# Attention with decay, first of four phases of a two-layer kernel: gates taken before the high part of the normed output, that part in four pieces, decay tables in two parts, the state updated with one kind of operation

## The reference, cut to what matters

```python
q = silu(x @ Wq); k = silu(x @ Wk); v = silu(x @ Wv)        # 2 x 1024 tokens, 16 heads of 32
D = exp(ld * (i - j)) * (i >= j)                             # inside a chunk of 128 tokens
q_decay = exp(ld * (i + 1)); k_decay = exp(ld * (127 - i)); chunk_decay = exp(ld * 128)
for each chunk:                                              # S starts at 0 in each sequence
    o = ((q @ k.T) * D) @ v + (q @ S) * q_decay
    S = chunk_decay * S + (k * k_decay).T @ v
gate = (x @ Wg1) @ Wg2
o = o * sigmoid(gate)
o = o * rsqrt(mean(o * o, per head) + 1e-5) * norm_w
x = layernorm(x + o @ Wo)
```

## Time and profile before

| | |
|---|---|
| median of 3 runs | 2120.58 us (2118.43 to 2133.62) |
| the profiled execution | 2121.79 us, its span 2120.0 us, granted clock 0.972 |
| attention phase | 0 to 378.3 us of the span |
| its round FIRST, chunks of t = 0 | 0 to 68.6, 68.6 to 95.2 us |
| a round NEXT and its chunks (t = 1) | 95.2 to 160.6, 160.6 to 180.4 us |
| the trunk | 378.3 to 2120.0 us |
| busy over the span | PE 88%, DVE 69%, POOL 61%, ACT 44% |

### The profile page before, as it was taken

One profiled execution on the slowest core, in us unless ns is written; L12 is line 12 of the kernel. 1 busy time (PEld: TensorE's weight loads), 2 busy tenths in 40 slices (PEclk: granted clock), 3 DMA queues, 4 the chain that ended last, 5 costly groups with the idle time before them and its releaser, 6 DMA issues. The chain is left out here.

```text
span 2120.0 us, 27907 instructions
## 1 busy us (share of the span) xinstructions
PE 1866.6 (88%) x9488; PEld 1184.6 (56%) x9488; DVE 1458.1 (69%) x1779; ACT 942.8 (44%) x1561; POOL 1296.3 (61%) x983
## 2 busy tenths in 40 slices
PE   8688897689998898888889889898998898999997
PEld 5556655357855555454545445454555455557785
DVE  2524414243337998798997999889989899994333
ACT  4333242344245555554546544564554544442212
POOL 4322520237327997788886998678878787782110
PEclk9899999899999999999999999999999999999999
DMA  6010100457667896778776886567657576764451
GB/s 207 22 40 2 41 20 11 150 179 267 227 214 265 322 328 235 252 268 295 267 266 224 314 297 223 193 231 253 224 205 274 192 251 225 260 222 159 166 210 61
DMA packets 132779, 427.28 MB, mean 202 GB/s; under 512 B 29184, under 2 KB 35840, under 8 KB 115872
## 3 DMA queue, kind: packets, MB, share of 16 engines
q1 hardware_dynamic: 132640, 425.53, 57.0%
HBM read 356.27 MB, written 69.21 MB: 201 GB/s over the span
## 5 line engine op out<-in xcount | busy, mean ns | idle before, releaser
L1489 POOL TENSOR_TENSOR h_times_c<-h_states,c_rep 128x512 f32<-128x512 f32 x512 | 669.7, 1321 | 177.7 <-PE scan_y L1137 118.4
L1271 ACT ACTIVATE decay<-delta_on_states,a_neg 128x512 f32<-128x512 f32 x512 | 353.7, 692 | 455.0 <-DVE h_states L1399 413.7
L1349 DVE TENSOR_TENSOR x<-x,y_or_aux 128x512 f32<-128x512 f32 x256 | 173.6, 678 | 221.8 <-PE y_or_aux L80 221.8
L1457 POOL TENSOR_TENSOR h_lo<-silu_in_h_lo,h_hi 128x512 fp32r<-128x512 f32 x128 | 171.3, 1338 | 248.0 <-ACT h_hi L1194 247.4
L1128 PE MATMUL du_spread<-stack,selectors 96*128 96x512 bf16 x512 | 203.0, 397 | 107.2 <-DVE d_b L1379 79.5
L1379 DVE TENSOR_TENSOR d_b<-du_spread,b_rep 128x512 f32<-128x512 f32 x384 | 254.7, 663 | 9.8 <-PE du_spread L1128 9.8
L78 PE MATMUL y_or_aux<-h_hi,w 128*128 128x512 f32 x512 | 241.6, 472 | 21.2 <-ACT b_rep L1236 8.9
L78 PE MATMUL gate<-x_hi,w 128*128 128x512 f32 x512 | 253.6, 495 | 7.4 <-POOL x_lo L1462 5.2
L1399 DVE TENSOR_TENSOR_SCAN h_states<-decay,h_last,d_b 128x512 f32<-128x512 f32 x192 | 245.1, 1277 | 12.8 <-ACT decay L1271 8.0
L78 PE MATMUL up<-x_hi,w 128*128 128x512 f32 x512 | 247.8, 484 | 0.0
L1399 DVE TENSOR_TENSOR_SCAN h_states<-decay,d_b 128x512 f32<-128x512 f32 x192 | 233.4, 1216 | 16.1 <-ACT decay L1271 11.7
(11 more groups left out here) (149 smaller groups left out, 3244.8 us busy)
## 6 DMA issues: line engine op xcount, KB each, us to landing
delta_on_states<-delta SPq DMA_DIRECT2D x256, 512.0 KB, 6.0
w<-w_split SPq DMA_DIRECT2D x112, 1024.0 KB, 6.7
w<-w_split SPq DMA_DIRECT2D x112, 512.0 KB, 6.4
w_split<-w_presplit SPq DMA_DIRECT2D x48, 512.0 KB, 5.6
w_split<-w SPq DMA_DIRECT2D x16, 1024.0 KB, 6.2
h_times_c<-in_w13a SPq DMA_DIRECT2D x16, 512.0 KB, 4.2
w_split<-w SPq DMA_DIRECT2D x16, 512.0 KB, 6.3
w_presplit<-in_w13b SPq DMA_DIRECT2D x32, 256.0 KB, 5.1
```

The lines of the kernel that those rows point to most:

```text
L1271: act.activation(da[:, s % ND], dring[:, s % NR], ACT.Exp, scale=a[:, column(s):column(s) + 1]).then_inc(s_da, 1)
L1349: dve.tensor_tensor(xt, xt, bank[:, :], ALU.add).then_inc(s_bank, 1)
L1457: pool.tensor_tensor(hl[:, idx % 4], sg[:, idx % 4], hh[:, idx % 4].bitcast(F32), ALU.subtract).then_inc(s_hl, 1)
L1489: pool.tensor_tensor(hc[:, s % NC_], hs[:, s % NH], crep[:, tile_of(s // SPO) % 2], ALU.mult).then_inc(s_hc, 1)
```

## The change

Five things are changed, all in the attention phase.
1. In FIRST, `decays` is cut in two: half of D, half of q_decay, k_decay and chunk_decay after the first take of k; the rest after the first take of v. Before it ran after the gate.
2. In NEXT, ACT takes the four gate products first and makes the high part of the normed output after them, in four casts of 128x512; DVE makes the low part in four pieces, each when its high piece is there; PE's first `wo` product waits for them piece by piece.
3. POOL makes the low part of the next x in four pieces.
4. The state's two operations per chunk become four `scalar_tensor_tensor` operations (128x32 each, one per feature tile), whose second tensor is in PSUM and whose scalar is one column of chunk_decay in SBUF.
5. Semaphores follow (counts in `on_hi`, `on_lo`, `attn_xl`; `state_scaled` is gone).

```diff
                     def outputs():
-                        if items is not TAIL:
-                            pe.wait_ge(s_ol, t)
                         for m in range(KD):
-                            project("wo", 3, m, onh, onl,
-                                    (lambda k: [by_piece(k, s_ol, NT, p_ol)]) if items is TAIL and m == 0 else None)
+                            project("wo", 3, m, onh, onl, (lambda k: [(s_ol, KD * rd.prev + k + 1)]) if m == 0 else None)
...
-                        pe.wait_ge(s_xl, t + 1)
+                        pe.wait_ge(s_xl, KD * t + 1)
...
-                def decays():
+                def decays(part):
...
-                    for j in range(HPT):
+                    for j in range(HPT)[2 * part:2 * part + 2]:
...
-                    for m in range(KD):
+                    for m in range(KD)[2 * part:2 * part + 2]:
...
                     def high_of_normed():
...
-                        act.wait_ge(s_on, KD * t + 1)
-                        act.wait_ge(s_pj, rd.done("v", CPT - 1))
-                        act.copy(onh[:, :, :], on[:, :, :]).then_inc(s_oh, 1)
+                        act.wait_ge(s_pj, rd.base if items is TAIL else rd.done("v", CPT - 1))
+                        for k in range(KD):
+                            act.wait_ge(s_on, KD * rd.prev + k + 2)
+                            act.copy(onh[:, k], on[:, k]).then_inc(s_oh, 1)
...
-                    take("k", kT, ACT.Silu)
+                    take("k", kT, ACT.Silu, ms=range(1))
+                    if items is FIRST:
+                        decays(0)
+                    take("k", kT, ACT.Silu, ms=range(1, KD))
...
-                    take("v", v, ACT.Silu)
+                    take("v", v, ACT.Silu, ms=range(1))
+                    if items is FIRST:
+                        decays(1)
+                    take("v", v, ACT.Silu, ms=range(1, KD))
+                    if items is NEXT:
+                        act.wait_ge(s_on, KD * t + 1)
+                    take("gate", sig, ACT.Tanh, 0.5)
                     if items is NEXT:
                         high_of_normed()
-                    take("gate", sig, ACT.Tanh, 0.5)
                     if items is FIRST:
-                        decays()
...
-                    pool.tensor_tensor(xl[:, :, :], x[:, :, bass.ts(t, TT)], xh[:, :, :].bitcast(F32),
-                                       ALU.subtract).then_inc(s_xl, 1)
+                    for k in range(KD):
+                        pool.tensor_tensor(xl[:, k], x[:, k, bass.ts(t, TT)], xh[:, k].bitcast(F32),
+                                           ALU.subtract).then_inc(s_xl, 1)
...
+                    def low_of_normed():
+
+                        for k in range(KD):
+                            dve.wait_ge(s_oh, KD * rd.prev + k + 1)
+                            dve.tensor_tensor(onl[:, k], on[:, k], onh[:, k].bitcast(F32), ALU.subtract).then_inc(s_ol, 1)
...
-                        dve.tensor_tensor(st[:, :, :], st[:, :, :], cdec[:, :].unsqueeze(2).to_broadcast([P, KD, HD]),
-                                          ALU.mult).then_inc(s_us, 1)
-                        dve.wait_ge(s_us, n + 1)
-                        dve.tensor_tensor(st[:, :, :], st[:, :, :], u_ps[:, :, :], ALU.add).then_inc(s_st, 1)
+                        for m in range(KD):
+                            mm = dve.scalar_tensor_tensor(out=st[:, m], in0=st[:, m], scalar=cdec[:, m:m + 1],
+                                                          in1=u_ps[:, m], op0=ALU.mult, op1=ALU.add)
+                        mm.then_inc(s_st, 1)
```

More of the change, by code:

```diff
@@ L139, in attention_phase @@
         s_o, s_og = p.sem("o_done"), p.sem("og_ready")
-        s_u, s_us, s_st = (p.sem(n) for n in ("update_done", "state_scaled", "state_ready"))
+        s_u, s_st = (p.sem(n) for n in ("update_done", "state_ready"))
         s_sq, s_sd, s_on = (p.sem(n) for n in ("squares", "head_rstd_ready", "on_ready"))
@@ L148, in attention_phase @@
         s_w0 = [p.sem(f"attn_w0_in_piece{k}") for k in range(KD)]
-        p_xh, p_xl, p_wh, p_wl, p_sq, p_oh, p_ol = (p.sem(f"attn_{n}_piece") for n in (
-            "xh", "xl", "w_hi", "w_lo", "squares", "on_hi", "on_lo"))
+        p_xh, p_xl, p_wh, p_wl, p_sq = (p.sem(f"attn_{n}_piece") for n in ("xh", "xl", "w_hi", "w_lo", "squares"))
         def by_piece(k, whole, count, piece):
@@ L422, in weight_high @@
                     act.copy(aw_hi[:, i], raws[i % 2][:, :, :]).then_inc(s_wh, 1)
-                def decays():
-                    act.wait_ge(s_sm, 96)
-                    act.wait_ge(s_const, 16)
-                    for j in range(HPT):
+                def decays(part):
+                    if part == 0:
+                        act.wait_ge(s_sm, 96)
+                        act.wait_ge(s_const, 16)
+                    for j in range(HPT)[2 * part:2 * part + 2]:
                         for m in range(KD):
@@ L432, in decays, with take @@
                                            scale=ldt[:, h:h + 1]).then_inc(s_dexp, 1)
-                    for m in range(KD):
+                    for m in range(KD)[2 * part:2 * part + 2]:
                         act.activation(qdec[:, m, :], const[:, C_POS:C_POS + P], ACT.Exp,
                                        scale=ldf[:, m:m + 1]).then_inc(s_dexp, 1)
-                    act.activation(kdec[:, :], kdec[:, :], ACT.Exp,
-                                   scale=const[:, C_REV:C_REV + 1]).then_inc(s_dexp, 1)
-                    act.activation(cdec[:, :], ldf, ACT.Exp, scale=float(CH)).then_inc(s_dexp, 1)
+                    if part == 0:
+                        act.activation(kdec[:, :], kdec[:, :], ACT.Exp,
+                                       scale=const[:, C_REV:C_REV + 1]).then_inc(s_dexp, 1)
+                        act.activation(cdec[:, :], ldf, ACT.Exp, scale=float(CH)).then_inc(s_dexp, 1)
                 def body(rd):
                     t, items = rd.t, rd.items
-                    def take(name, out, f, scale=1.0):
-                        for m in range(KD):
+                    def take(name, out, f, scale=1.0, ms=range(KD)):
+                        for m in ms:
                             act.wait_ge(s_pj, rd.done(name, m))
@@ L590, in body @@
                                                      in1=sq[:, m], op0=ALU.mult, op1=ALU.mult).then_inc(s_on, 1)
-                        if items is TAIL:
-                            for k in range(KD):
-                                dve.wait_ge(*by_piece(k, s_oh, NT, p_oh))
-                                dve.tensor_tensor(onl[:, k], on[:, k], onh[:, k].bitcast(F32), ALU.subtract)\
-                                   .then_inc(by_piece(k, s_ol, NT, p_ol)[0], 1)
+                    def low_of_normed():
+                        for k in range(KD):
+                            dve.wait_ge(s_oh, KD * rd.prev + k + 1)
+                            dve.tensor_tensor(onl[:, k], on[:, k], onh[:, k].bitcast(F32), ALU.subtract).then_inc(s_ol, 1)
                     def add_outputs():
@@ L604, in body @@
                     if items is TAIL:
+                        low_of_normed()
                         add_outputs()
```

9 lines of the change are left out of this document (removed).

## The result

The changed kernel took 2114.64 us (median of 14 runs) beside 2129.14 for the kernel before (median of 14): ratio 0.9942, 95% interval 0.9923 to 0.9961, that is 12 us less (8 to 16; the medians are 14.5 apart). Timed again on another chip it gave the same ratio, 0.9942 (0.9925 to 0.9960). The forecast was 11.3 us less than the profiled execution, which is 0.9947, and 2110 us in all. The kernel before ranges from 2118 to 2134 as in the three runs that I had seen, but the median of 14 is 2129.14, where that of the three was 2120.58: my forecast started too low.

What follows compares the result with a forecast made beforehand. It took waits in the attention phase as all the change could move, on POOL and ACT; the trunk keeps its length. Gains 5.5 + 1.3 + 4.5 = 11.3 us off 2121.79 gave 2110 us, range 2102 to 2119.

Steps and rivals of the forecast that it cites:

- The state, 5.5 us: First tile's first chunk: the new state operations do not wait for POOL, so the stall goes; 5.5 us gained.
- The decays, 1.3 us: First tile: with decays in two parts, scores start at 68.1 instead of 68.62 and take about 0.9 less; 1.3 us gained.
- PE slips 2.0 us: First tile, PE's fourth k product: its bank is freed at 33.0 instead of 31.0, after the first decays part.
- Rival (b): First tile: three more table loads cost 1.4 us more each, so POOL starts still later; 2113 us, 8%.
- rival (d): First tile: DVE's mask and q_decayed slip between POOL's stages cheaply, PE stays at 2.4 GHz; 6 us more, 2104, 13%.
- The table loads gone from the loop, zero: ACT in the loop: removed loads lay in covered waits, so nothing gained; without that cover 2.6 us a tile.
- The loop, 4.5 us: Other three tiles: low pieces let POOL's last butterfly end earlier; 1.5 us a tile taken, 4.5 in all.
- my two cases: POOL's last butterflies in the loop: first low piece comes between them, gain 1.24 us a tile, or misses, 1.9.
- rival (c): Loop: low pieces hold POOL as long as before, or PE falls to 1.2 GHz more often; gain 0, 2115, 18%.
- The trunk: From 378.3 us on, 1741.7 us long: keeps its length; a change over 3 us would show the forecast wrong.
- Rival (a): Chunks of the first three tiles: new state operations wait for POOL too; 47 us lost, 2163 us, 4%.

Runs made afterwards that it cites:

- state only: Kernel before, with only the state's two operations per chunk replaced by four that read the update from PSUM; ratio to before 0.9979.
- decays only: Kernel before, with only the decays cut in two parts, after the first takes of k and of v; ratio to before 1.0060.
- load kept: Kernel before with the decays' split, plus one table load put back ahead of the next tile's cast in the loop; ratio to before 1.0012.
- all but decays: Changed kernel with the decays in one piece again, after the gate; ratio to before 0.9932, taken again 0.9939.
- gates only: Kernel before, with only the loop's gates taken first and the normed output's high and low parts in four pieces; ratio to before 0.9976.
- x low pieces only: Kernel before, with only POOL's low part of x in four operations and PE's wait for them; ratio to before 0.9987.

## Why the prediction was right, by its own steps

**The state, 5.5 us.** Measured 5.5 (state only: 94.55 to 89.08). My own numbers gave 5.6 (84.86 less 79.26). The mechanism was right: these operations, with one tensor in SBUF, one in PSUM and a column in SBUF, took 0.71 or 0.72 us beside POOL and without it. Four operations cost 0.71 us, where I took 1.0. What I missed is that cutting POOL's operation gives the same in the first tile; two parts of the change remove the same stall, so their gains alone (5.5 each by the second gated output) don't add.

**The decays, 1.3 us.** The gain was not found, and one step was off in size: "PE slips 2.0 us". PE waited 2.04 us, but in the first profile fell to 1.2 GHz behind it and slipped 3.8; POOL's second load and its butterflies came 4.7 later instead of 2.0. In the second profile the clock stayed and the step was right (2.3). Decays only has the one case (its first transform at 38.84), load kept the other (37.44), so it changes from run to run. The other terms stood: 6.3 us for the first part (6.4 forecast), 4.2 us (4.7 forecast) that DVE's operations add to POOL, a transform at 1.2 GHz after 5 us of idle. In the profile of the changed kernel the first `probs` came 0.4 us later than before instead of 1.3 earlier, in its second 1.5 earlier; and without the split the time is the same within what the runs can tell. Rival (b) fell by the loads' rows, and rival (d) by POOL's 3.35 and 3.40.

**The table loads gone from the loop, zero.** Right for this kernel and for a reason that I had not given. ACT has time for them, but POOL's low part of x starts 1.3 us earlier without them. With the old state operation the kernel without them has a phase 9.3 us longer (decays only), of which one load put back undoes 7.4 (load kept). With the new operation no state operation waits, and the changed kernel and all but decays, which keeps the loads, are alike.

**The loop, 4.5 us.** POOL's end moved by 1.32, 1.95 and 2.05 us, 5.3 in sum, at the upper end of my two cases and a little above; for the idle at 1.2 GHz I had nothing, and the fourth tile gained 2.6 by it, the third lost 1.5. Of rival (c) the half on the clock is real: in the profile of gates only it took 2.2 of the 5.5 us by which POOL's end had moved.

**The trunk.** I had said wrong if its length changed by more than 3 us. It did, by 7. But over 13 profiles its length lies between 1741 and 1749 us, with 1745.5 and 1748.1 for kernels whose phase is nearly that of before, 1741.1 and 1740.9 for others. So it is within the spread of the trunk, and the 1741.6 that I started from was at its lower end. Both profiles of the changed kernel lie at the upper end, 1748, so a small share of its own is not excluded; but the ratio, 12 us less, leaves no room for 7 us lost in every run beside a phase 10 to 11 us shorter. What sets the length was not tested: PE's busy time there, 1552.6 to 1563.9 us, follows it only loosely. The profile's span, 2116.9, contains this 7 us, which is why it missed the 2108.7.

**The sum.** The forecast of 11.3 us was right, in part by luck: the decays' 1.3 us can't be found in the times, and the loop gave 0.8 more than I took. The absolute forecast of 2110 lay 4.6 us below the 2114.64 measured.

Rival (a) fell by the first profile: no state operation waited.

## What to carry to other kernels

Before a step is called free because its engine has time, look at what it delays: here a table load of 1.28 us kept POOL 0.08 us behind a DVE operation, and without the load, with the old state operation, that kernel was 0.6% slower. An operation with two SBUF inputs beside a busy POOL, here 0.28 to 6.26 us, is worth turning into one with an input from PSUM, here 0.71 us for four at every place. Where PE idles for some 2 us at a fixed place, count the idle and a possible fall of the clock behind it, here 2.3 or 3.8 us for the same wait, and first try to give PE the next products of its own list: putting kT ahead of the transform took 11.9 us from the three loop tiles in the profiles, though four runs of each kernel don't yet settle what of it the time keeps.

## What the runs showed that I had not expected

- A 2.04 us idle of PE was followed by 3.5 to 3.7 us at 1.2 GHz in two profiles (the changed kernel's first, decays only) and by none in two others (its second, load kept), at the same place and after the same work; an idle of 3.23 us, in the second tile, was followed by none either.
- In the kernel before, the waiting DVE operation was not served at the ends of two POOL operations that followed one another (73.23 to 79.49). The same happened in decays only (252.73 to 258.73) and, with POOL's work in four pieces, once in x low pieces only (165.71 to 168.74); at other places, as 164.06 to 167.60 in decays only, it was served at the first end.
- The `tensor_scalar` that halves `nw` (128x4, line 578) took 1.15 us beside POOL, and 0.17 where POOL was idle (line 577 before): it has a single SBUF tensor and was longer all the same.
